# Attention on one core: a new order of values, maxima and side jobs between the score matmuls

## The reference, cut to what matters

```python
q = (x @ Wq).reshape(b, n, N_HEADS, HEAD_DIM)
k, v = jnp.split(ctx @ Wkv, 2, axis=-1)
q = apply_axial_rope(q, pos_map)
k = apply_axial_rope(k, ctx_pos_map)
logits = jnp.einsum('bqhd,bkhd->bhqk', q, k) * scale
w = jax.nn.softmax(logits, axis=-1)
attn = jnp.einsum('bhqk,bkhd->bqhd', w, v)
attn = attn.reshape(b, n, N_HEADS * HEAD_DIM)
return attn @ Wout + bout
```

## Time and profile before

| | us |
|---|---|
| median of 3 runs | 1476.78 (1474.0 to 1477.7) |
| the profiled execution | 1476.94 |
| its span, first to last instruction | 1475.3 |
| attention, first score to the last values | 797.28 to 1308.92 |
| reduces of maxima, first and last start | 755.9 to 1268.5 |
| TensorE busy, share of the span | 81% |
| granted TensorE clock, mean | 0.90 |

### The profile page before, as it was taken

One profiled execution on the slowest core, in us unless ns is written; L12 is line 12 of the kernel. 1 busy time (PEld: TensorE's weight loads), 2 busy tenths in 40 slices (PEclk: granted clock), 3 DMA queues, 4 the chain that ended last, 5 costly groups with the idle time before them and its releaser, 6 DMA issues. The chain is left out here.

```text
span 1475.3 us, 16906 instructions
## 1 busy us (share of the span) xinstructions
PE 1193.5 (81%) x5316; PEld 516.5 (35%) x5317; DVE 862.7 (58%) x1314; ACT 649.1 (44%) x1143; POOL 399.3 (27%) x474
## 2 busy tenths in 40 slices
PE   2757566769997999994335998999999999995897
PEld 2333333345553444442101322322232222232453
DVE  4585858551243555521558888777777777416543
ACT  1333232345541222225502766656666666734443
POOL 0505051501113222211453433222222330005332
PEclk8777787889998999998566999999999999996999
DMA  5141312244324444434353333222232220007011
GB/s 199 44 143 32 126 55 73 80 164 155 116 86 171 143 144 151 152 102 163 101 172 104 98 96 106 84 70 81 70 93 84 70 81 24 2 0 87 29 44 44
DMA packets 106355, 141.56 MB, mean 96 GB/s; under 512 B 20788, under 2 KB 75572, under 8 KB 106280
## 3 DMA queue, kind: packets, MB, share of 16 engines
q1 hardware_dynamic: 87912, 111.77, 23.0%
q0 software_dynamic: 18368, 28.85, 7.5%
HBM read 97.44 MB, written 46.27 MB: 97 GB/s over the span
## 5 line engine op out<-in xcount | busy, mean ns | idle before, releaser
L2236 DVE TENSOR_REDUCE a_top<-PS 128x2 f32<-128x1024 f32 x256 | 308.3, 1222 | 100.3 <-PE PS L2010 96.0
L2094 ACT ACTIVATE a_E<-PS 128x512 f32<-128x512 f32 x512 | 277.7, 596 | 157.4 <-PE PS L1993 157.2
L1993 PE MATMUL PS<-a_Q,a_K 99*128 99x512 bf16 (+1 forms) x512 | 167.4, 387 | 16.6 <-ACT a_E L2094 6.5
L1251 PE MATMUL PS<-f_W,f_GT 128*128 x312 | 142.3, 599 | 0.0
L2010 PE MATMUL PS<-a_K,a_Q 64*128 64x512 bf16 x512 | 104.4, 405 | 46.0 <-DVE a_top L2236 27.7
L2023 PE MATMUL PS<-a_E,a_V 128*32 128x512 f32 x1024 | 137.2, 608 | 0.0
L1993 PEld LDWEIGHTS PS<-a_Q,a_K 99*128 99x128 bf16 (+1 forms) x512 | 44.3, 97 | 156.1 <-ACT a_E L2094 104.5
L1642 POOL TENSOR_TENSOR a_qf<-a_qf,a_tab 128x512 f32<-128x512 f32 x16 | 20.7, 1294 | 275.8 <-DVE a_swapped L2185 275.7
L1307 DVE TENSOR_TENSOR f_H<-f_SG,PS 128x256 f32<-128x256 f32 x39 | 16.4, 421 | 125.8 <-ACT f_SG L1291 125.8
L1251 PEld LDWEIGHTS PS<-f_W,f_GT 128*128 128x128 f32 x312 | 57.1, 193 | 57.6 <-issue 57.6
L1938 PE MATMUL PS<-a_xT,a_wq 128*128 128x512 f32 x128 | 74.1, 676 | 2.2 <-ACT a_xT L2064 0.8
(11 more groups left out here) (354 smaller groups left out, 2015.4 us busy)
## 6 DMA issues: line engine op xcount, KB each, us to landing
f0r_raw<-in_L_ffn_W_dram SPq DMA_DIRECT2D x24, 512.0 KB, 5.2
a_K<-k_parts SPq DMA_DIRECT2D x192, 64.0 KB, 2.3
a_Q<-a_q_parts SPq DMA_DIRECT2D x192, 64.0 KB, 2.5
f_y<-f_Y SPq DMA_DIRECT2D x39, 256.0 KB, 2.0
v_units<-V SPq DMA_DIRECT2D x16, 512.0 KB, 3.7
a_V<-v_units SPq DMA_DIRECT2D x16, 512.0 KB, 3.4
k_parts<-f_k_parts SPq DMA_DIRECT2D x16, 384.0 KB, 3.4
a_q_parts<-a_parts SPq DMA_DIRECT2D x16, 384.0 KB, 2.7
```

The costliest lines, as they stand in the source:

```text
L1251: last = nc.tensor.matmul(PS[:, 2 + k % 2, 0:2 * I], GT[k][:, c, :], W13[:, bass.ds(e, 1), c, :].rearrange("p a n -> p (a n)"), start=(c = ...
L1993: nc.tensor.matmul(PS[:, 4 + h % 2, :], K6[k][0:rows_, o, head // 2, kt * P:(kt + 1) * P], Q6[k][0:rows_, o, head // 2, :], start=True, st ...
L2094: nc.scalar.activation(E[step % 2][:, h, :], PS[:, 4 + h % 2, :], ACT.Exp).then_inc(exp_done, 1)
L2236: nc.vector.tensor_reduce(top[:, h - h % 2:h - h % 2 + 2, t], PS[:, 2 * pair:2 * pair + 2, :], AX.X, ALU.max).then_inc(maxed, 1)
```

## The change

It moves work, and computes the same. On TensorE the values stand between the two pairs of scores, behind the even slot, and both maxima behind the second pair. On ACT take_sum comes before exps 2 and 3. The table of jobs is laid out anew for c = 0 turns and for the others. The maxima run two heads ahead of the turn instead of four (`AHEAD = 2`): in steps 0 and 1 heads 6 and 7 of the next unit, in steps 2 to 7 heads 0 to 5 of the one behind it. On DVE outs(n) comes before the reduce at even n; cut_max moves from n = 7 to n = 3, the swap from 5 to 6; normalising and add_bias go by tiles, at 8 to 11 and 12 to 15 (in b = -1 turns all normalising at 7); ACT's square root moves to step 0 in the b = -1 turns. Code of SP and POOL stays as it is.

```diff
             crowded = c == 0
-            for d, when in enumerate((0, 0, 1, 2) if crowded else (0, 1, 2, 3)):
+            for d, when in enumerate((0, 0, 1, 1) if crowded else (0, 1, 2, 3)):
                 add(when, "q", before(b, c, -3), d)
-            add(3 if crowded else 4, "o", before(b, c, 1), 1)
-            add(5 if crowded else 6, "a", before(b, c, 1))
-            add(9, "m", before(b, c, -1))
             if crowded:
-                for d, when in enumerate((6, 7, 8, 10)):
-                    add(when, "x", (b + 1, 0), d)
-            add(11 if crowded else 10, "o", (b, c), 0)
-            for d, when in enumerate((13, 14, 15, 15) if crowded else (12, 13, 14, 15)):
+                add(2, "x", (b + 1, 0), 0)
+                add(3, "x", (b + 1, 0), 1)
+            add(4, "o", before(b, c, 1), 1)
+            add(6, "a", before(b, c, 1))
+            add(7, "m", before(b, c, -1))
+            if crowded:
+                add(8, "x", (b + 1, 0), 2)
+                add(9, "x", (b + 1, 0), 3)
+            for d, when in enumerate((10, 11, 12, 12) if crowded else (9, 10, 11, 12)):
                 add(when, "p", (b - 1, 0), (c, d))
+            add(14, "o", (b, c), 0)
...
+        AHEAD = 2
+
         def max_heads(b, c):
 
-            return [(before(b, c, -1), 4 + st) if st < 4 else (before(b, c, -2), st - 4) for st in range(8)]
+            return [(before(b, c, -1), HU - AHEAD + st) if st < AHEAD else (before(b, c, -2), st - AHEAD) for st in range(8)]
...
                     scores((b, c), step, 0)
                     scores((b, c), step, 1)
-                    maxima(*heads[step], 0)
                     slot(2 * step)
-                    scores((b, c), step, 2)
-                    scores((b, c), step, 3)
-                    maxima(*heads[step], 1)
                     if step == 0:
                         values(before(b, c, 1), 7)
                     else:
                         values((b, c), step - 1)
+                    scores((b, c), step, 2)
+                    scores((b, c), step, 3)
+                    maxima(*heads[step], 0)
+                    maxima(*heads[step], 1)
                     slot(2 * step + 1)
...
-                    if step == 3 and nb is not None:
+                    if step == (0 if b == -1 else 3) and nb is not None:
...
                     exps((b, c), step, (0, 1))
                     slot(2 * step)
-                    exps((b, c), step, (2, 3))
                     if step == 0:
                         take_sum(before(b, c, 1), 1)
                     if step == 4:
                         take_sum((b, c), 0)
+                    exps((b, c), step, (2, 3))
...
                     at(4, aggregate)
-                    at(8, normalize)
-                    at(12, add_bias)
+                    at(7, normalize)
+                    for t in range(TB):
+                        at(7 if b == -1 else 8 + t, lambda t=t: normalize_tile(t))
+                        at(12 + t, lambda t=t: add_bias(t))
...
-                    at(5, swap)
+                    at(6, swap)
...
-                    at(7, cut_max)
+                    at(2 * AHEAD - 1, cut_max)
...
+                    if n % 2 == 0:
+                        outs(n)
                     if is_unit(*unit):
...
-                    outs(n)
+                    if n % 2:
+                        outs(n)
```

More of the change, by code:

```diff
@@ L2165, in normalize, with normalize_tile, add_bias @@
                             v.wait_ge(xT_ready, nb * DC)
[L2166 to L2175, removed]
+                    def normalize_tile(t):
+                        one = nc.vector.tensor_scalar(xh[:, t, :], X[:, nb * TB + t, :], mv[:, t, 0:1], rstd[:, t:t + 1],
+                                                      ALU.subtract, ALU.mult)
+                        if t == TB - 1:
+                            one.then_inc(xh_ready, 1)
+                    def add_bias(t):
+                        if t == 0:
+                            v.wait_ge(xh_ready, nb + 1)
+                        nc.vector.tensor_tensor(X[:, nb * TB + t, :], X[:, nb * TB + t, :], tbias[:], ALU.add).then_inc(bias_added, 1)
+                        if t == TB - 1:
+                            v.wait_ge(bias_added, (nb + 1) * TB)
                     at(4, aggregate)
-                    at(8, normalize)
-                    at(12, add_bias)
+                    at(7, normalize)
+                    for t in range(TB):
+                        at(7 if b == -1 else 8 + t, lambda t=t: normalize_tile(t))
+                        at(12 + t, lambda t=t: add_bias(t))
                 q = before(b, c, -3)
```

## The result

The changed kernel takes 1495.62 us (median of 4 runs, 1492.38 to 1498.49) against 1476.47 for the kernel before: ratio 1.0134, 95% interval [1.012, 1.0148]. Run again on another chip it took 1493.0, ratio 1.0104 [1.0086, 1.0122]. It is slower, as forecast, but by more: 1486.3 with a range to 1495 was predicted, which the first median misses by 0.6 us. The profiled execution took 1492.38 (span 1490.8), 15.4 over that of before where the sum said +9.4.

The account below looks back on a forecast made before the run. Each turn takes the longer of TensorE's work and the chain from DVE's swap through POOL to the m rows, which mostly rules; attention +5.6 and start +3.8 give +9.4, so 1486.3 us, range 1472 to 1495 with the rivals.

Parts of the forecast that it names:

- the swap decides: Middle turns: swap at 17.1 us instead of 13.4, rows of maxima landing at 32.95, spending the room of 3.1.
- plain steps: TensorE steps without a side job in the attention stage: 2.89 us instead of 3.21.
- the cut: DVE's cut_max at task 3, out of POOL's rotation: 1.07 us, against 2.47 beside it.
- Rival 1: Rows land before TensorE's work ends, so its order rules: middle turns 32.0, total 1464.6 us; chance 0.11.
- Rival 2: Swap shifts by 2.9 us instead of 3.7, in some eleven turns: 8.8 less, 1477.5 us; chance 0.14.
- The sum in attention: Turns 0 to 15, each the longer of TensorE's work and the side chain: 517.25 us, +5.6.
- Rival 3: Clock falls to 1.2 GHz in new waits starting turns 1 to 4, four at 1.8 us: 1493.5; chance 0.13.
- the argument from turn 3 of before: Turn 3 of the kernel before had waits similar to the new 2 to 3 us ones, at granted clock 1.00.
- the place of the swap there, 18.0: Turns 3 and 7: swap 18.0 us into the turn, giving turn lengths of 34.05 and 34.2.
- The start: First scores of attention near 801.05 instead of 797.28, with maxima two heads ahead: +3.8 us.
- Free, by little: At the start, unit 1's maxima can be reduced at 780, just ahead of 781, when DVE gets to them.
- Behind attention: Stages other than attention are not touched, and what they take stays.

Follow-up runs that it names:

- the control: Kernel before with only the m store and the two m loads moved from POOL's queue to SP's; 1477.65 us, ratio 1.0012.

## Why the prediction was right or wrong

*What bounds the kernel, and that the swap decides: right, and shown.* Late swap alone makes before slower; early swap, or rows that don't stand behind the rotation, makes after faster than before; and the control says before had the room. The predicted places held: swap 16.74 to 16.95 in middle turns (17.1), the next turn 15.3 to 16.0 behind it (15.85), plain steps 2.88 to 2.89 (2.89), the cut 1.07 (1.07), middle turns 32.06 to 32.77 (32.95), turns 13 to 15 81.42 (82.4).

*Rival 1, that the chain has room: false for this kernel, but its price was right.* It said 1464.6 for TensorE's own order; the kernels with the swap at 3 took 1465.56 to 1467.79, the one with only the rows on SP 1472.82. That the price came out is in part luck, as two errors in it cancelled: a middle turn without the chain is 31.06, not 32.0 (the two steps with two q jobs, for one, end at 9.04 where I summed 9.24), and turns 3 and 7 cost more. Rival 2, a smaller shift: false but for 0.4 us a middle turn.

*The sum in attention: +9.5 for +5.6.* Turn by turn of the first profile, measured less forecast:

| term | us |
|---|---|
| turns 1, 2: swap at 18.37 and 18.17 for 17.1 (clock falls) | +2.3 |
| turns 1, 2: rows 16.2 and 16.7 behind the swap for 15.95 | +1.0 |
| turn 3: swap at 22.41, where it is at 19.50 with the rows on SP (clock falls) | +2.9 |
| turns 3, 7: swap at 19.50 and 19.30 for 18.0 (table loads) | +2.8 |
| turn 7: rows 16.75 behind the swap for 16.2 (POOL waited 3.80 for the m store, for 2.9) | +0.6 |
| all the rest: turns 0, 4 to 6 and 8 to 15 (-5.0; swap 0.2 to 0.4 sooner, rows sooner behind it), turn 3's rows (-0.7) | -5.7 |

The errors do not all go one way: 9.6 us that the sum had put at nothing or too low stand against 5.7 that it had put too high, so the sum missed by less than its terms did.

*Rival 3, the clock: it came true, and I gave it 0.13.* Four falls at 1.8 us ahead of swaps were its price, and 1493.5 its time. In the trace there are five in attention, three of them 3.4 us long or more at the starts of turns 1 to 3, one later in turn 3, ahead of its swap as well, and one in turn 7 that had hardly begun at its swap. Falls ahead of swaps are 5.2 of the table, for the 7.2 of the rival; that its 1493.5 lies so near is partly luck, since it left out the table loads and the stages outside attention as the forecast did. The window of the first fall, and the scores that start turn 1, of the kernel after:

```profile
834.80:838.20 3.40, 3.18 (x11) 0.88 (x10) 0.35 (x1) 1.09 (x2) 0.16 (x1) 0.50 0.79 234
```

```profile
834.68 0.56 PE L1998 MATMUL PS<-a_Q,a_K 99*128 99x512 bf16 x1 [1.79 <-DMA a_Q<-a_m_rows]
```

0.50 is the lower of TensorE's two levels, 1.2 of 2.4 GHz. Turns 1, 2 and 3 waited 1.79, 3.31 and 3.75 for rows and all fell; middle turns waited 0.9 to 1.6 and didn't. The Trainium skill's page "TensorE: Matmul & The Clock Gate", section "HAM oscillation — how this bites in real kernels", tells of a kernel whose clock fell in each of its waits for DMA, of some 3 to 5 us; here it fell in shorter ones too, from 1.79 us. The step of the prediction that failed is the argument from turn 3 of before, by which the clock was left out of the sum: I wrote that this turn had waits like the new ones, of 2 to 3 us, at a clock of 1.00. Its longest unbroken wait of TensorE is 1.44:

```profile
905.60 0.88 PE L1993 MATMUL PS<-a_Q,a_K 99*128 99x512 bf16 x2 [1.44 <-ACT a_E L2094]
```

Its waits are for exps and for DVE's reduces, spread over the turn, and said nothing of one unbroken wait of TensorE at a turn's start.

*Turns 3 and 7, missed outright.* The forecast took 34.05 and 34.2 from the chain; they took 37.75 and 36.05. The same two loads are in the trace of before, and turns 3 and 7 stand out as long in the earlier trace rows (35.46 and 35.81); I let the chain set them and did not ask what made them long, so the second step that failed is the place of the swap there, 18.0, which has no term for them. In the new order step 3, where they stand, takes 6.3 to 7.1 us (3.64 without), ahead of the swap, so they enter the chain.

*The start: +4.3 for +3.8.* Counted from DVE's first reduce it is 47.7 instead of the 45.1 forecast (41.4 before); that the stages ahead ended 2.0 us sooner in this execution hid most of it. The swap of unit 2 is at 785.13 (784.9 forecast, from a first reduce 2.0 us later), behind a wait of 1.51 for TensorE's maxima:

```profile
776.89 1.23 DVE L2248 TENSOR_REDUCE a_top<-PS 128x2 f32<-128x1024 f32 x1 [1.51 <-PE PS L2015]
...
785.13 0.72 DVE L2195 STREAM_SHUFFLE a_swapped<-a_qf 128x512 f32<-128x512 f32 x1
```

"Free, by little", I wrote of those maxima; the margin was not there. With four heads ahead and the swap at 3 the same distance is 40.1: the cost is AHEAD's and the swap's.

*Behind attention: +1.7 for 0.* A stage that I took as untouched changed all the same. In the first profile of the kernel after, in those built on it but the one with only the rows on SP, and in the kernel before with the swap at 8, the clock falls within 5 us of the last values: the last p jobs behind attention take 16.93 us with the fall (swap at 3) and 13.97 without (rows on SP), and part of that is absorbed by a wait behind them; the tail is 167.7 to 168.6 us with it and 166.1 to 166.5 without. It is not the kernel's own: the second profile of the kernel after has no such fall, takes 13.97 for these jobs and has a tail of 166.1, with the same waits of TensorE (1.17, 0.80, 0.97 and 0.77) there. Why the fall comes in one execution and not in another, no run separates.

Sum, for the first profile: 9.4 + 3.9 (attention) + 0.5 (start) + 1.7 (behind) = 15.5.

## What to carry to other kernels

When an order of work on the bounding engine is improved, follow the engines that hang on it in program order: the first task on an in-order queue sets when everything behind it can go, and an unrelated transfer (here the m store, ready 8 us sooner) can be what pays. A side chain with room in a turn is a number (3.1 us and 1 us here) to subtract each shift from, and each wait it opens on TensorE has to be priced twice, once for itself and once for the clock that may fall behind it. If a task has to be late, move what is queued behind it to another queue; if it needn't be, move it first: the swap at task 3 turned +1.3% (+1.0% on another chip) into -0.7% and -0.6%.

## What the runs showed of the hardware

- A fall of the granted clock to 0.50 for 3.4 us cost 1.6 us of a chain of matmuls (turns 5 and 6 of the kernel before with the swap at 8). At the starts of turns 1 to 3 of the changed kernel it returned in the second profile; behind attention it did not. Waits for rows of 1.8 us and more at a turn's start brought one within 1.9 us of the first score, ahead of it or behind, in 12 of 13 cases (both profiles of the changed kernel, the kernel before with the swap at 8; a wait of 2.74 passed without), waits of 0.9 to 1.6 in none of 16 (the same, and the changed kernel with the swap at 5). Inside a turn a wait of 1.44 had a fall behind it (turn 7 of the kernel before, at 1042.0) and one as long had none (its turn 3), so the length of the one wait does not say it.
- Ln followed by Exp needs as many table loads as Sqrt between Exps in turns 3 and 7 here: 1.28 us each, two per turn, without a drain ahead of or behind them.
- POOL's rotation of 8.65 to 8.7 us was stretched to 9.24 between swap and store in turns 1 and 2 of the changed kernel, its last two operations from 0.62 and 1.16 to 0.86 and 1.47; what ran beside them was not separated.
